# Two graph stages whose last turn compares ahead of its sums and scatters by halves, and column loads placed ahead of waits

## The reference, cut to what matters

```python
# layers 0 and 1
msg = jax.nn.relu(x[src] + edge_attr)
agg = jax.ops.segment_sum(msg, dst, num_segments=N_NODES)
h = (x + agg) @ W1l + b1l
mu = jnp.mean(h, axis=0); var = jnp.mean(jnp.square(h - mu), axis=0)
h = jax.nn.relu((h - mu) * jax.lax.rsqrt(var + BN_EPS) * gl + bl)
h = jax.nn.relu(h @ W2l + b2l)
# layers 2 and 3
agg = jax.ops.segment_sum(x[src], dst, num_segments=x.shape[0])
h = (1.0 + eps) * x + agg
h = jax.nn.relu(h @ wA.T + bA) @ wB.T + bB
# around them: h = max(layernorm(x), 0); x = x + layers(h), twice
```

## Time and profile before

| | |
|---|---|
| median of 3 runs | 2802.92 us (2801.63 to 2803.49) |
| profiled execution, its own time | 2802.75 us |
| its span, first to last instruction | 2800.8 us |
| busy: PE, DVE, ACT, POOL | 1930.9, 1708.4, 744.5, 1946.8 us |
| layer 0: last gather issued, first dense product | 994.46, 1012.28 us |
| layer 1: last gather issued, first dense product | 2027.26, 2044.71 us |
| layers 2 and 3: first dense product | 2422.16, 2772.61 us |

### The profile page before, as it was taken

The page is one execution under the profiler, slowest core; times in us unless marked ns, Lnnn a source line. Parts: engine busy times, 40 slices in busy tenths (PEclk is TensorE's granted clock), DMA queues, the critical chain, the costliest instruction groups (busy, mean ns, idle before and its releaser), DMA issues.

```text
span 2800.8 us, 30306 instructions
## 1 busy us (share of the span) xinstructions
PE 1930.9 (69%) x9233; PEld 1259.2 (45%) x9233; DVE 1708.4 (61%) x2751; ACT 744.5 (27%) x1002; POOL 1946.8 (70%) x2060
## 2 busy tenths in 40 slices
PE   2565666666666663656666656556568999989998
PEld 2453444443444342444434444334344566545665
DVE  7887767677767644777777777777664222442222
ACT  4222222222223241333333333333351000120001
POOL 6777777777777717777777777777707777377773
PEclk8788788778787876888777888887878999999999
DMA  6343333434343432444444445454516665366653
GB/s 198 117 123 120 112 120 105 127 112 127 113 135 120 135 96 83 133 135 142 127 149 141 148 135 159 152 156 155 169 35 201 207 224 195 126 202 211 223 192 104
DMA packets 224862, 403.74 MB, mean 144 GB/s; under 512 B 41225, under 2 KB 129117, under 8 KB 224741
## 3 DMA queue, kind: packets, MB, share of 16 engines
q1 hardware_dynamic: 159204, 267.94, 27.8%
q0 software_dynamic: 65536, 134.35, 18.2%
HBM read 337.92 MB, written 64.21 MB: 144 GB/s over the span
## 4 chain that ended last, share of the span: by engine, by line
POOL 50%; PE 26%; issue 17%; DMA 4%; DVE 3%; ACT 1%; DVEq 1%; POOLq 0%; SPq 0%; ACTq 0%
POOL xg L559 50%; PE psA L1328 17%; PE psG L1343 4%; DMA xg<-node_table,src_all 3%; PE psG L1392 2%; PE psA L1400 1%; PE psG L1307 0%; DVE xp_room L955 0%; PE psG L1422 0%; DVE hid L1040 0%; PE psA L1409 0%; DVE acc L878 0%; DVE xp_room L803 0%; DMA hid<-in_src_dram 0%; DVEq L903 0%
## 5 line engine op out<-in xcount | busy, mean ns | idle before, releaser
L559 POOL DMA_INDIRECT xg<-node_table,src_all x1536 | 1452.3, 945 | 522.4 <-issue 461.3
L1307 PE MATMUL psG<-hid,xp_room 128*128 128x160 f32 x3136 | 611.7, 370 | 379.4 <-DVE hid L919 353.7
L1292 PE MATMUL psA<-cell_room,xp_room 128*128 128x512 f16 (+1 forms) x2176 | 574.2, 417 | 386.2 <-ACT count_out L626 270.1
L1307 PEld LDWEIGHTS psG<-hid,xp_room 128*128 128x128 f32 x3136 | 592.6, 249 | 432.0 <-issue 406.0
L947 DVE TENSOR_SCALAR cell_room<-psG,cell_all 128x980 f16<-128x980 int16 x1088 | 712.5, 713 | 0.0
L579 POOL DMA_INDIRECT xg<-node_table,idx x480 | 461.2, 961 | 271.6 <-issue 267.4
L634 ACT COPY psG<-xp_room 128x512 f32<-128x512 f32 x384 | 226.4, 590 | 1266.8 <-DVE xp_room L955 1248.5
L1292 PEld LDWEIGHTS psA<-cell_room,xp_room 128*128 128x128 f16 x2176 | 218.6, 106 | 696.0 <-ACT count_out L626 303.6
L955 DVE TENSOR_TENSOR xp_room<-psG,xg 128x512 f32<-128x512 f32 x384 | 262.4, 683 | 438.3 <-DMA xg<-node_table,src_all 435.2
L878 DVE TENSOR_TENSOR acc<-acc,product 128x40 f32 x192 | 39.0, 203 | 396.5 <-ACT product L686 372.0
L919 DVE SCALAR_TENSOR_TENSOR hid<-loc_all,round_off,psG 128x2560 f32<-128x2560 f32 x98 | 280.4, 2861 | 0.0
(11 more groups left out here) (141 smaller groups left out, 762.2 us busy)
## 6 DMA issues: line engine op xcount, KB each, us to landing
xp_room<-in_edge_attr_dram SPq DMA_DIRECT2D x98, 768.0 KB, 4.7
cell_room<-count_store SPq DMA_DIRECT2D x16, 3000.0 KB
count_store<-count_out SPq DMA_DIRECT2D x96, 490.0 KB, 3.1
hid<-count_store SPq DMA_DIRECT2D x16, 2880.0 KB
xp_room<-in_edge_attr_dram SPq DMA_DIRECT2D x98, 256.0 KB, 5.1
xg<-node_table,src_all POOLq DMA_INDIRECT x1536, 2.5
node_table<-rows_h SPq DMA_DIRECT2D x48, 256.0 KB, 2.3
xg<-node_table,idx POOLq DMA_INDIRECT x480
```

What stands on the lines that cost most here:

```text
L559: nc.gpsimd.indirect_dma_start(xg[:, n % 2, u, j, :], None, x if n < RAW_TURNS else table, bass.IndirectOffsetOnAxis(ap=src_all[:, s, j:j ...
L1292: last = nc.tensor.matmul(psA[:, bank, 0:w], src_hot[:, hots(n) % 2, i, :], cells[:, c % CELL_RING, c0:c0 + w], start=(c == first), stop=( ...
L1307: last = nc.tensor.matmul(psG[:, q, h * WIN:(h + 1) * WIN], ea[:, t, u, j, :], hot[:, q, u, j, :], start=(u == slots[0] and j == 0), stop= ...
```

## The change

1. In the last turn of layers 0 and 1, `windows_of` (the adds of turn n-2, the columns, the compare) stands ahead of the turn's sums, once. Its one-hots go to `last_hot`, a part of `cell_room`, so DVE first waits for `cells_used` of the layer. PE reads them there.
2. Behind the sums come `add_windows` of the turn before, then a loop over the rounds that adds the last turn's windows and compares for the next round. With one round this is one compare that nothing multiplies; it reads its row of numbers from `iota_c` in SBUF, not from PSUM. `round_off` gets one more column for it. `spare_sets` counts this extra signal, and SP waits for it ahead of the first load of counts.
3. `add_windows` and `add_late_windows` read both columns into registers ahead of the wait for PE's products, in all turns; at the end of layers 2 and 3 the columns of both last turns are read ahead of everything (`late_columns`).

```diff
+        last_hot = cell_room[:, 0:2 * SLOTS * EPP * WIN].bitcast(F32).rearrange("p (u j w) -> p u j w", u=SLOTS, j=EPP)
...
             sp.wait_ge(cells_used, CHUNKS)
+            sp.wait_ge(hot_set[1], sp.snap(rounds * TURNS + 1))
...
-            def add_windows(q, uses, adds):
-
+            def first_columns(q):
+
+                dve.sem_inc(windows_opened, 1)
+                return [dve.value_load(first_i[0:1, q, h:h + 1], min_val=0, max_val=NODES) for h in range(WINDOWS)]
+
+            def add_windows(layer, q, uses, adds):
+
+                dve.wait_ge(firsts_set[q], dve.snap(uses + (spare_sets(layer, q) + 1)))
+                firsts = first_columns(q)
                 dve.wait_ge(scattered[q], dve.snap(uses + 1))
-                dve.wait_ge(firsts_set[q], dve.snap(uses + 1))
-                dve.sem_inc(windows_opened, 1)
-                for h in range(WINDOWS):
-                    first = dve.value_load(first_i[0:1, q, h:h + 1], min_val=0, max_val=NODES)
-
+                for h, first in enumerate(firsts):
                     dve.wait_ge(window_added, dve.snap(adds + h + 1))
                     window_add(psG[:, q, h * WIN:(h + 1) * WIN], first, WIN).then_inc(window_added, 1)
...
-                for n in range(layer * TURNS, (layer + 1) * TURNS):
+                final = (layer + 1) * TURNS - 1
+                for n in range(layer * TURNS, final + 1):
                     chunk_rows(n)
+                    if n == final:
+                        dve.wait_ge(cells_used, LAYER_CHUNKS[layer + 1])
+                        windows_of(layer, n, dve.snap(rounds * 0), last_hot)
                     for u in range(SLOTS):
                         for c in slot_chunks(n, u):
                             chunk_cells(c)
                         if n > RAW_TURNS:
                             slot_sum(n, u)
-                    with dve.Fori(0, rounds) as r:
-                        windows_of(layer, n, r)
+                    if n < final:
+                        with dve.Fori(0, rounds) as r:
+                            windows_of(layer, n, r, hot[:, n % 2, :, :, :])
...
+                q = 1 - final % 2
+                add_windows(layer, q, dve.snap(rounds * ((final + 2 - q) // 2)),
+                            dve.snap(rounds * (final * WINDOWS) + (2 * layer + 1) * WINDOWS))
+                with dve.Fori(0, rounds) as r:
+                    add_windows(layer, final % 2, dve.snap(rounds * (final // 2) + r + 1),
+                                dve.snap((rounds * final + r) * WINDOWS + (2 * layer + 2) * WINDOWS))
+                    set_windows(final, dve.snap(r + 1), last_hot, iota_c)
...
+                firsts = [late_columns(q, uses[q]) for q in range(2)]
+                add_late_windows(1, uses[1], end, firsts[1])
                 add_units(layer, pairs, dve.snap(end + WINDOWS))
-                add_late_windows(0, uses[0], dve.snap(end + (WINDOWS + UPG)))
+                add_late_windows(0, uses[0], dve.snap(end + (WINDOWS + UPG)), firsts[0])
...
             def edge_windows(layer, n):
 
                 q, t = n % 2, n % RING
+                rows = last_hot if n == (layer + 1) * TURNS - 1 else hot[:, q, :, :, :]
                 with pe.Fori(0, rounds) as r:
-                    pe.wait_ge(hot_set[q], pe.snap(rounds * (n // 2) + r + 1))
+                    pe.wait_ge(hot_set[q], pe.snap(rounds * (n // 2) + r + (spare_sets(layer, q) + 1)))
```

More of the change, by code:

```diff
@@ L123 @@
 LAYERS = 4
+assert TURNS % 2 == 1 and 2 * SLOTS * EPP * WIN <= CELL_RING * CB
 assert SUPERS % SLOTS == 0 and OVERLAP % EPP == 0 and SECOND <= P
@@ L171, in gnn_kernel @@
         iota_c = sb("iota_c", [P, IOTA], I16)
-        round_off = sb("round_off", [P, BLOCKS])
+        round_off = sb("round_off", [P, BLOCKS + 1])
         ones_row = sb("ones_row", [1, P])
@@ L404, in groups_before, with spare_sets @@
             return (layer - 2) * (pairs + 1)
+        def spare_sets(layer, q):
+            return 1 if layer == 1 and q == (TURNS - 1) % 2 else 0
         def pair_adds(rounds):
@@ L919, in windows_of @@
                 nc.vector.scalar_tensor_tensor(
-                    out=hot[:, q, :, :, :].rearrange("p u j w -> p (u j) w"),
+                    out=rows.rearrange("p u j w -> p (u j) w"),
                     in0=loc.unsqueeze(2).broadcast_to((P, SLOTS * EPP, WIN)),
                     scalar=round_off[:, bass.DynSlice(r, 1)],
-                    in1=iota_bank[:, 0:WIN].unsqueeze(1).broadcast_to((P, SLOTS * EPP, WIN)),
+                    in1=iota[:, 0:WIN].unsqueeze(1).broadcast_to((P, SLOTS * EPP, WIN)),
                     op0=ALU.subtract, op1=ALU.is_equal).then_inc(hot_set[q], 1)
@@ L972, in edges, with late_columns, add_late_windows @@
                             slot_sum(RAW_TURNS, u)
-                end = (layer + 1) * TURNS
-                for h, q in enumerate((end % 2, 1 - end % 2)):
-                    turns = (end + 1 - q) // 2
-                    add_windows(q, dve.snap(rounds * turns), dve.snap(rounds * (end * WINDOWS) + (2 * layer + h) * WINDOWS))
-            def add_late_windows(q, uses, adds):
+                q = 1 - final % 2
[5 more added lines that the diff above has]
+                    set_windows(final, dve.snap(r + 1), last_hot, iota_c)
+            def late_columns(q, uses):
+                dve.wait_ge(firsts_ready[q], dve.snap(uses + 1))
+                return first_columns(q)
+            def add_late_windows(q, uses, adds, firsts):
                 dve.wait_ge(reduced[q], dve.snap(uses + 1))
-                dve.wait_ge(firsts_ready[q], dve.snap(uses + 1))
-                dve.sem_inc(windows_opened, 1)
-                for h in range(WINDOWS):
-                    first = dve.value_load(first_i[0:1, q, h:h + 1], min_val=0, max_val=NODES)
+                for h, first in enumerate(firsts):
                     dve.wait_ge(added, dve.snap(adds + (h + 1)))
@@ L1149, in _ @@
             dve.wait_ge(more_consts, 3)
-            link(nc.vector.tensor_scalar(reached_f[:, :], round_off[0:1, :], plan_f[:, 0:1], None, ALU.is_le))
+            link(nc.vector.tensor_scalar(reached_f[:, :], round_off[0:1, 0:BLOCKS], plan_f[:, 0:1], None, ALU.is_le))
             link(nc.vector.tensor_reduce(plan_f[:, 1:2], reached_f[:, :], AX_X, ALU.add))
@@ L1307, in edge_windows @@
                                 last = nc.tensor.matmul(
-                                    psG[:, q, h * WIN:(h + 1) * WIN], ea[:, t, u, j, :], hot[:, q, u, j, :],
+                                    psG[:, q, h * WIN:(h + 1) * WIN], ea[:, t, u, j, :], rows[:, u, j, :],
                                     start=(u == slots[0] and j == 0), stop=(u == slots[-1] and j == EPP - 1))
```

15 lines of the change are left out of this document (8 added, 7 removed).

## The result

The changed kernel takes 2780.24 us (median of 6 runs, 2776.51 to 2783.02) beside 2802.8 us for the kernel before (6 runs, 2801.63 to 2804.51) on the same chip: ratio 0.9917, 95% interval 0.9907 to 0.9927, or 22.6 us less.

A forecast was written before the change was run, and what follows sets the result against it. It took the exposed handovers at layer ends as the bound: gains of 7.1, 8.4, 1.1 and 2.1 us in layers 0 to 3, together 18.7, from 2802.75 to 2784.05, so 2784; range 2780.5 to 2790.

The forecast's parts named there:

- Compare ahead and scatter by halves: Ends of layers 0 and 1: only 16 records, 4.2 us, follow the last relu; gains 6.9 and 5.7 us.
- first rival: Layers 0 and 1: PE still starts all 32 records after the last relu; 12.8 us gained, 2789.9; chance 0.07.
- Nothing lost ahead: Last turn: the earlier compare delays the first sum some 4 us, covered by the second slot's gather; nothing or tenths lost.
- Column loads, 1.1 and 1.4: PE's scatter end to dense product, layers 0 and 1: loads ahead of the waits gain 1.1 and 1.4 us.
- Extra compare, 0 after 1.2 us of delay: Behind the last add, layers 0 and 1: first statistics 1.2 us late, made up over 12 groups; cost 0.
- Load of counts: SP's first load, issued about 2040 instead of 2017.85: cost 0, and layer 1's last gather lands 0.5 us sooner.
- The clock: PE's granted clock at the dense parts: layer 0 loses 0.9 us, layer 1 gains 0.8, layer 2 0, layer 3 gains 1.0.
- other three clock terms: Dense parts: layer 0 loss 0.9 us (bound 3.0), layer 1 gain 0.8 (+1.7, -1.3), layer 3 gain 1.0 (0 to 2.7).
- Layer 0's loss of 0.9: Layer 0's dense part, perhaps starting slow: the middle between no loss and layer 1's 1.7 us.
- the third: Slow dense starts in layers 0 and 1, no clock gain in layer 3: 13.5 us gained, 2789.3; chance 0.12.
- the five gains: Column loads in all four layers and layer 1's faster gather: 1.1 + 1.4 + 0.5 + 1.1 + 1.1, given as 5.1 us.
- the case that was left out: Layers 0 and 1: both second scatter halves at full clock (4 us more) and both dense parts fast; 2777.5.

The follow-up runs named there:

- one-piece kernel: The changed kernel with PE waiting for both relus of the last turn before scattering anything; 2783.29 us, ratio 0.9932.
- ten idle products: The kernel before with ten unread products ahead of the wait for the last adds in layers 2 and 3; 2796.9 us, ratio 0.9984.
- the repeat: The changed kernel run once more with nothing altered, for the spread and a second trace; 2780.77 us, ratio 0.9918.
- three with idle products: The changed kernel with unread products between the last scatter's halves, ahead of second and first counts products, or both; 2774.7, 2772.48, 2771.33 us on usual chips.
- first set of idle products: The changed kernel with 20 unread products between the halves of the last scatter of layers 0 and 1; 2774.7 us, ratio 0.9908 on a usual chip.

## Why the prediction was nearly right, and the step that failed

- **Compare ahead and scatter by halves: right.** Last relu's end to the scatter's end: 4.40 us in layer 0 (1000.02 to 1004.42) and 4.43 in layer 1, forecast 4.3; gains of 6.9 and 5.6 against 6.9 and 5.7. The slow rate was taken from the earlier trace rows and measured 4.35 and 4.38. The one-piece kernel prices the first rival's mechanism: 2.0 and 2.3 us, where its terms said 3.0 and 1.9.
- **Nothing lost ahead: right.** The compare ends at 987.49, forecast about 986.5 for gathers that are issued 1.1 earlier; the first sum starts there, the second slot's at 988.75, against the gathers no later than before, and the third waits for its own.
- **Column loads, 1.1 and 1.4: right** (pauses 2.18 to 1.10 and 2.53 to 1.09). In layer 3 1.13 came; in layer 2 1.6, for with the loads went a gap of 0.43 us too, which the chain of the kernel before shows as "issue" at the end of the unit adds (2419.56).
- **Extra compare, 0 after 1.2 us of delay: right.** It takes 2.87 us; the dense product to the second product is 14.74 us with and without it. Leaving it out gave no gain.
- **Load of counts: right.** Issued at 2032.36, forecast near 2033; the last gather lands in 2.53 us. Alone the effect is below what the runs can tell.
- **The clock: the step that failed.** The prediction took 0 for layer 2, "since DVE adds the last bias over all rows behind its last add, and what the dense part could gain waits for that". The bias pass holds only the first groups. In the kernel before DVE's results then come one by one, each after a wait for PE (the first two of the timeline of layer 2's end; the fourth stands 12.34 us behind the dense product, in the changed kernel 9.67):

```profile
2428.91 0.75 DVE L1099 TENSOR_SCALAR acc<-psA,bias_second 128x512 f32<-128x512 f32 x1 [0.21 <-PE psA L1400]
2430.62 0.75 DVE L1099 TENSOR_SCALAR acc<-psA,bias_second 128x512 f32<-128x512 f32 x1 [0.97 <-PE psA L1400]
```

In the changed kernel PE is ahead and three results stand in one row of 2.06 us (above, 2409.11); DVE makes up the backlog, and the layer is 2.7 us shorter. The ten idle products, which move no load and no add, give the same 2.7 us, so the term was real in the kernel before. The mistake is to take a long pass as cover for all that is queued behind it, where the queue behind it has slack. With 2.7 in the place of 0 the sum is 21.4 and the forecast 2781.4; the range's low end comes out as the good bounds of the other three clock terms together, and it had none for this one.
- **The other clock terms.** Layer 3's dense part gained 1.7 where 1.0 was taken (bound 2.7). That term compared "two gaps near 2.2", but the 2.14 was counted from L982; PE's own pause ahead of layer 3 was 2.62 us, and ahead of layer 2 3.09. Layer 0's loss of 0.9 didn't come in the first profile. Layer 1 gained 1.7, but its start, like layer 0's, is fast or slow for a reason that the traces don't show: of the eight profiles of the changed kernel and its variants on usual chips (the first, the repeat, without loads ahead, whole scatter, no extra compare, three with idle products) layer 0 started slow in two and layer 1 in three. So in the median these two terms are a mean over such starts, and that the sum came near is in part luck. The 0.9 us of each second product had no term either. And the rise of the clock moved at the first counts products of layer 3, 1.3 us that no term had. Windows of 2 us from there, before and after:

```profile
2463.86:2465.86 2.00, 2.00 (x6) 0.75 (x7) 2.00 (x2) 0.59 (x2) 1.70 (x2) 0.50 0.16 39
2465.86:2467.86 2.00, 2.00 (x7) 0.76 (x6) 2.00 (x2) 1.00 (x1) 1.67 (x2) 0.50 0.16 35
```

```profile
2441.69:2443.69 2.00, 2.00 (x6) 0.76 (x7) 2.00 (x2) 0.59 (x2) 1.70 (x2) 0.50 0.18 41
2443.69:2445.69 2.00, 2.00 (x10) 0.89 (x9) 2.00 (x2) 0.99 (x1) 1.67 (x2) 0.82 0.14 33
```

The clock rises one window earlier, and 16 records stand in 4 us in place of 13. The 75 records take 16.69 us instead of 17.98, and 16.68 in the repeat, but 18.11 without the extra compare and 17.77 with the first set of idle products. What moves the rise was not tried.
- **The rivals.** Slow starts of both dense parts (the third) occur in single executions and cost 1.6 and 1.9 us each; for layer 3 that rival's condition never came. In the first rival's sum the five gains are 5.2, not 5.1, and the case that was left out comes to 2778.2 by its own terms, not 2777.5; neither moves the forecast. The Trainium skill (TensorE: Matmul & The Clock Gate, HAM oscillation) warns of idle gaps in which PE falls back to half rate, and the prediction read it as a slow start for both dense parts. The traces agree for the second half of the scatter (4.35 us behind 6.10 idle, 2.44 with idle products) and not for the pauses of 1.48, behind which the granted clock stayed at 1.00; that section's case is a long wait for data in each turn of a loop, not a pause as short as these.

## What to carry to other kernels

Read the granted clock behind every pause of PE on the critical path, before and after an edit: here 4.4 us of the gain, at layers 2 and 3, are shown to be the clock's, and idle products in the pauses that were left gave some 8 us more. A pause at one length kept the clock in one execution and lost it in the next, so judge by more than one profile. A long pass on another engine covers an earlier arrival only if that engine has no slack behind it; look for the "idle before" of its next instructions. Idle products must end before the work they keep warm is ready, and where arrival times differ between chips they can become the delay.

## What the runs showed that was not expected

The same gather takes 0.94 us of POOL or up to 1.47, by whether DVE's multiply of two SBUF tiles is already running when it starts. In the changed kernel's start the first gather below starts just ahead of such a multiply, the second 0.07 us behind one, and the next gather then starts 1.75 instead of 1.25 us later:

```profile
32.44 0.95 POOL L566 DMA_INDIRECT xg<-in_x_dram,src_all  x1 [0.30 <-issue]
...
33.62 0.69 DVE L839 TENSOR_TENSOR rows_h<-rows_h,ln_rstd 128x512 f32<-128x512 f32 x1 [0.47 <-ACT rows_h L614]
33.69 1.45 POOL L566 DMA_INDIRECT xg<-in_x_dram,src_all  x1 [0.30 <-issue]
```

Where a gather starts beside a running multiply of this kind, it ends 0.82 us behind the multiply's end (1.45 us here, 1.23 in the kernel before, where less of the multiply was left). No run moves the multiply, so the cause is read from this pattern and not tested. Such gathers move the whole chain by about 1 us; with gathers of layer 1 that take 977.4 to 979.4 us and the two dense starts they are what differs most between the profiles of one kernel.

On the two slow chips PE waited for nothing that the profile shows for hundreds of us (groups of waits, the changed kernel; "issue" is a wait for nothing that the profile shows; the kernel before on a usual chip has 0.2 us of that kind at the scatter):

```profile
PE psA L1317 <- issue: 410.6, 218, 11.0
PE psG L1333 <- issue: 223.9, 149, 22.2
```

Single products start 0.7 to 2.8 us apart there. The stretches at the ends of layers 2 and 3 are the same as on the other chips (39.05 and 26.51 us), so PE's own rate is not lower in them; the cause was not settled.
